# Opening loads on the sync queue in order of use, and new order lists for all engines, in an adaLN + expert + SwiGLU kernel

## What is computed

```python
def layer0(x, mu):                       # mu: cond_512, 64 numbers per sequence
    U = (mu @ W_dec + b_dec).reshape(B, 129, 30)
    param = einsum('bik,kj->bij', U, V)
    y = einsum('bsd,bde->bse', x, param[:, :-1]) + param[:, -1][:, None]
    gate = y @ Wg.T + bg                 # top 2 of 8 experts, softmax of the two
    o = gelu(y @ W1[e].T + b1[e]) @ W2[e].T + b2[e]
    return x + sum(w[e] * o[e] for e in top2)

def layer1(x):                           # norms with table rows by token, three state MLPs
    c = mlp_ln(concat(w0*h, w1*t, w2*m, w3*n, w4*r, w5*s))
    g = silu(w1(c)) * w2(c)
    return x + w3(gelu(h2(gelu(h1(g)))))
```

## Time and profile before

| | |
|---|---|
| median of 3 runs | 432.87 us (432.76 to 434.07) |
| the profiled execution | 432.91 us |
| its span | 431.1 us |
| PE busy | 413.5 us, 96% |
| DVE, ACT, POOL busy | 73%, 68%, 27% |
| moved by DMA | 45.07 MB |

### The profile page before, as it was taken

The page is one execution under the profiler, slowest core; times in us unless marked ns, Lnnn a source line. Parts: engine busy times, 40 slices in busy tenths (PEclk is TensorE's granted clock), DMA queues, the critical chain, the costliest instruction groups (busy, mean ns, idle before and its releaser), DMA issues.

```text
span 431.1 us, 5758 instructions
## 1 busy us (share of the span) xinstructions
PE 413.5 (96%) x1812; PEld 270.2 (63%) x1812; DVE 312.8 (73%) x656; ACT 292.0 (68%) x518; POOL 115.0 (27%) x122
## 2 busy tenths in 40 slices
PE   8698899999999999999999999999999999898996
PEld 5475455544656765776567665776577556677774
DVE  5489999987995587658866657678864788666653
ACT  4378967877756874677746884686668474857654
POOL 0026401443426520244153000448035031110000
PEclk9999999999999999999999999999999999999999
DMA  7976637563453342324531160325502210000000
GB/s 235 361 326 175 191 102 190 131 177 98 134 122 106 105 127 65 105 52 119 150 92 38 49 172 2 87 62 172 164 0 65 73 56 0 2 0 26 0 24 27
DMA packets 30216, 45.07 MB, mean 105 GB/s; under 512 B 3717, under 2 KB 22634, under 8 KB 29674
## 3 DMA queue, kind: packets, MB, share of 16 engines
q1 hardware_dynamic: 25504, 32.82, 26.4%
q0 software_dynamic: 3584, 10.49, 7.5%
q10 hardware_dynamic: 1098, 1.40, 1.1%
HBM read 40.68 MB, written 4.03 MB: 104 GB/s over the span
## 4 chain that ended last, share of the span: by engine, by line
PE 78%; DVE 9%; DMA 4%; issue 4%; ACT 3%; ACTq 1%; POOL 1%; SPq 1%; DVEq 0%
PE bank L750 21%; PE bank L648 20%; PE bank L786 7%; PE bank L696 7%; PE bank L640 6%; PE bank L735 5%; PE bank L664 2%; PE bank L703 2%; DMA keepP<-keepP_in 2%; DMA t_split<-tsS 2%; PE bank L775 1%; DVE mG L1190 1%; ACT mG L899 1%; PE bank L555 1%; DVE bn L1199 1%
## 5 line engine op out<-in xcount | busy, mean ns | idle before, releaser
L648 PE MATMUL bank<-mG,W 128*128 128x512 f32 x256 | 119.6, 593 | 0.0
L899 ACT ACTIVATE mG<-bank,keepP 128x512 f32<-128x512 f32 x128 | 85.3, 687 | 27.2 <-PE bank L640 17.6
L1464 POOL TENSOR_TENSOR rstd<-ve,mhalf 128x4 f32<-128x4 f32 x24 | 32.8, 1366 | 203.6 <-DVE ve L1205 203.5
L1190 DVE TENSOR_TENSOR mG<-mG,gwbs 128x1024 f32<-128x1024 f32 x64 | 77.3, 1218 | 2.1 <-DMA gwbs<-gate_w 1.3
L648 PEld LDWEIGHTS bank<-mG,W 128*128 128x128 f32 x256 | 47.5, 189 | 38.9 <-issue 35.3
L640 PE MATMUL bank<-ts,A 96*128 96x512 f32 x128 | 62.2, 526 | 1.7 <-ACT mG L899 1.6
L964 ACT ACTIVATE G<-bank,keepP 128x512 f32<-128x512 f32 x48 | 32.2, 692 | 27.9 <-PE bank L750 27.8
L1445 POOL DMA_INDIRECT gp<-pgb_in,ixall x32 | 35.8, 1119 | 26.7 <-issue 9.1
L750 PE MATMUL bank<-hB_h,h2w_h 128*128 128x512 f32 x96 | 39.7, 414 | 0.0
L750 PE MATMUL bank<-hA_h,h1w_h 128*128 128x512 f32 x96 | 38.7, 403 | 0.0
L1448 POOL DMA_INDIRECT gcm<-ctm,ixcm x32 | 35.1, 1098 | 9.8 <-issue 9.4
(11 more groups left out here) (243 smaller groups left out, 782.4 us busy)
## 6 DMA issues: line engine op xcount, KB each, us to landing
gwbs<-gate_w SPq DMA_DIRECT2D x32, 512.0 KB
keep<-xT_in SPq DMA_DIRECT2D x8, 256.0 KB, 6.0
outT<-keep SPq DMA_DIRECT2D x8, 256.0 KB, 2.1
t_split<-tsS SPq DMA_DIRECT2D x7, 192.0 KB
ts<-t_split SPq DMA_DIRECT2D x7, 192.0 KB
W1T<-W1T_in SPq DMA_DIRECT2D x1, 1024.0 KB, 8.7
W<-W2T_in SPq DMA_DIRECT2D x1, 1024.0 KB, 13.6
hs<-h1T_in SPq DMA_DIRECT2D x1, 1024.0 KB, 8.5
```

The lines of the kernel that those rows point to most:

```text
L648: mm = pe.matmul(OACC[:, :], W2[:, e * HC + c, :], mG[n % NMG][:, c, :], start=False, stop=(e == E - 1 and c == HC - 1))
L899: act.activation(mG[e % NMG][:, c % HC, :], HM[n % 2][:, :], ACT.Gelu, bias=b1c[:, c:c + 1]).then_inc(m_gelu, 1)
L1190: dve.tensor_tensor(mine, mine, gate.unsqueeze(1).broadcast_to([P, HC, TT, P]), ALU.mult).then_inc(m_q, 1)
L1464: step(pool.tensor_tensor(rstd[:, n, :], ve[:, n, :], mhalf[:, :], ALU.pow))
```

## The change

Three things, in the opening's loads and in the lists:

1. Loads that ACT issued (bdec, Vk, keepP, wd_u, earlyP, w12s) are issued by SP; ACT keeps the two factors in `gap`, muT and bdec_u, the last now ahead of its first activation. SP's loads stand in a new order, W1T in two parts (its first 512 columns with a semaphore of their own). wd_u shares `ld_v` with Vk and keepP, so those who wait for one wait for all three.
2. The lists of all five engines are new, in every block. The weights are split in another order (w12, w3, h2, h1).
3. The change is said to have "seven products without readers". `WARM` and the four `fi` are the same in both programs; the `fi` stand at other places.

```diff
             load(Wd[:, :], A["W_dec"][:, 0:KR * D].rearrange("m (h c) -> m h c", h=2), ld_wd)
+            load(bdec, A["b_dec"][:, 0:KR * D].rearrange("o (i k) -> (o i) k", k=KR), ld_bd)
             load(keep[0][:, :], A["xT"][:, 0:T], x_in[0])
-            load(W1T[:, :], A["W1T"], ld_W1T)
+            load(Vk[:, :], A["V"], ld_v)
+            load(keepP[:, :], A["keepP"], ld_v)
+            load(wd_u, A["W_dec"][:, KR * D:KR * (D + 1)].unsqueeze(1).broadcast_to([MU, 2, KR]), ld_v)
+            load(W1T[:, 0:T], A["W1T"][:, 0:T], ld_W1T)
+            load(earlyP[:, :], A["earlyP"], ld_small)
+            load(keep[1][:, :], A["xT"][:, T:2 * T], x_in[1])
+            load(states[:, :, :], A["states"], ld_state)
+            load(earlyB[:, :], A["earlyB"].partition_broadcast(P), ld_state)
             sp.wait_ge(setup0, 1)
...
+            load(keep[2][:, :], A["xT"][:, 2 * T:3 * T], x_in[2])
+            load(W1T[:, T:], A["W1T"][:, T:], ld_W1T_rest)
+            load(xTr[0][:, :], A["xT"][:, 3 * T:5 * T], ld_x[0])
+            load(xTr[1][:, :], A["xT"][:, 5 * T:8 * T], ld_x[1])
...
-            load(W2[:, :, :].rearrange("p n d -> p (n d)"), A["W2T"], ld_w2)
-            load(w3s[:, :], A["w3T"], ld_w[3])
             sp.wait_ge(u_even, 4)
             sp.wait_ge(u_odd, 4)
             load(h1s, A["h1T"], ld_w[1])
+            load(W2[:, :, :].rearrange("p n d -> p (n d)"), A["W2T"], ld_w2)
             load(h2s, A["h2T"], ld_w[2])
+            load(w12s[:, :], A["w12T"], ld_w[0])
+            load(w3s[:, :], A["w3T"], ld_w[3])
             run(steps, ORDER["SP"])
...
                 elif n == 1:
+                    pe.wait_ge(ld_W1T_rest, 16)
                     pe.wait_ge(u_odd, 1)
...
-            load(wd_u, A["W_dec"][:, KR * D:KR * (D + 1)].unsqueeze(1).broadcast_to([MU, 2, KR]), ld_wu)
-            load(bdec, A["b_dec"][:, 0:KR * D].rearrange("o (i k) -> (o i) k", k=KR), ld_bd)
-            load(Vk[:, :], A["V"], ld_v)
-            load(keepP[:, :], A["keepP"], ld_v)
-            load(earlyP[:, :], A["earlyP"], ld_small)
+            load(bdec_u, A["b_dec"][:, KR * D:KR * (D + 1)].rearrange("o k -> k o"), ld_bd)
             act.wait_ge(setup0, 1)
             act.activation(warmA[:, 0:64], onesf[:, 0:64], ACT.Copy)
-            load(bdec_u, A["b_dec"][:, KR * D:KR * (D + 1)].rearrange("o k -> k o"), ld_bd)
...
-            load(w12s[:, :], A["w12T"], ld_w[0])
...
-            dve.wait_ge(ld_wu, 16)
+            dve.wait_ge(ld_v, 48)
```

Of the lists, SP's of block 0 and PE's of block 6:

```diff
-                (0, "sgw0 sgp0 sts1 gb0 lr gb1 +lt sts2 sts3 gb2 gb3 sgw1 sgp1"),
+                (0, "sts1 sgw0 sgp0 sts2 gb0 +lt lr gb1 gb2 gb3 sgw1 sgp1"),
...
-                (6, "H0 -O5 H1 H2 ~F1 H3 =Ts H4 -O6 =Th H5 ~F2 H6 -O7 =Z B H7 ~F3 O0 H8 H9 -XT =Y ~F4 ~F5 ~F6 ~F7 H10 O1 H11 =YT O2 "
-                    "H12 ~F8 ~F9 ~F10 ~F11 H13 O3 O4 ~F12 H14 =F0 -Tt H15"),
+                (6, "H0 H1 =Ts -O5 H2 H3 =Th ~F1 H4 -O6 -O7 ~F2 =Z ~F3 -XT H5 H6 =Y B O0 H7 ~F4 ~F5 ~F6 ~F7 H8 -Tt H9 O1 =YT O2 H10 "
+                    "~F8 ~F9 H11 H12 ~F10 ~F11 H13 O3 H14 O4 ~F12 H15 =F0 -Ts"),
```

More of the change, by code:

```diff
@@ L222, in build @@
         CT = nc.dram_tensor("ctm", [A["ctg"].shape[0] * A["msg"].shape[0], 3 * P], F32, kind="Internal").ap()
-        ld_v, ld_wd, ld_wu, ld_bd, ld_small, ld_W1T, ld_const, ld_state = sems("ld_v", "ld_wd", "ld_wu", "ld_bd", "ld_small", "ld_W1T", "ld_const", "ld_state")
+        ld_v, ld_wd, ld_bd, ld_small, ld_W1T, ld_W1T_rest, ld_const, ld_state = sems(
+            "ld_v", "ld_wd", "ld_bd", "ld_small", "ld_W1T", "ld_W1T_rest", "ld_const", "ld_state")
         ld_x = sems("ld_x0", "ld_x1")
@@ L305, in weights_done @@
         def weights_done(eng, *ns):
-            eng.wait_ge(w_lo, max((4, 2, 1, 3)[n] for n in ns))
+            eng.wait_ge(w_lo, max((4, 3, 2, 1)[n] for n in ns))
         def wide(v, n):
@@ L332, in build @@
             "ACT": (
[19 rows of a table removed]
[19 rows of a table added]
             ),
             "DVE": (
[14 rows of a table removed]
[15 rows of a table added]
             ),
             "POOL": (
-                (0, "tcl0 ix tcl1 tcl2 tab0 srt tab1 tab2 tab3 rt0"),
-                (1, "tab0 -rt1 tab1 tab2 rt0 tab3 -rt2 rt1"),
-                (2, "tab0 tab1 tab2 rt0 tab3"),
-                (3, "tab0 =rt2 -rt1 tab1 tab2 tab3 rt0"),
-                (4, "tab0 =rt2 tab1 -rt1 tab2 tab3"),
-                (5, "tab0 -rt0 tab1 tab2 =rt2 -rt1 -rt2 tab3 rt0 rt1"),
-                (6, "tab0 tab1 tab2 tab3"),
-                (7, "tab0 -rt0 -rt1 =rt2 tab1 tab2 -rt2 tab3 rt0 rt1 rt2"),
[8 rows of a table added]
             ),
             "SP": (
[8 rows of a table removed]
[4 rows of a table added]
+                (4, "gb0 ^stored -lx -li gb1 gb2 +lt gb3 +lr ~stored #lt"),
[3 rows of a table added]
             ),
@@ L428, in _ @@
                 load(dst, A[src], ld_state)
-            load(states[:, :, :], A["states"], ld_state)
-            load(earlyB[:, :], A["earlyB"].partition_broadcast(P), ld_state)
+            load(keep[2][:, :], A["xT"][:, 2 * T:3 * T], x_in[2])
+            load(W1T[:, T:], A["W1T"][:, T:], ld_W1T_rest)
+            load(xTr[0][:, :], A["xT"][:, 3 * T:5 * T], ld_x[0])
+            load(xTr[1][:, :], A["xT"][:, 5 * T:8 * T], ld_x[1])
             nm, nc_ = A["msg"].shape[0], A["ctg"].shape[0]
@@ L520, in _ @@
                      "sgp": lambda i, g: store_parts(g), "vts": lambda i: store_terms(), "vtl": lambda i: load_terms()}
-            for b in (1, 2):
-                load(keep[b][:, :], A["xT"][:, b * T:(b + 1) * T], x_in[b])
-            load(xTr[0][:, :], A["xT"][:, 3 * T:5 * T], ld_x[0])
-            load(xTr[1][:, :], A["xT"][:, 5 * T:8 * T], ld_x[1])
-            load(W2[:, :, :].rearrange("p n d -> p (n d)"), A["W2T"], ld_w2)
-            load(w3s[:, :], A["w3T"], ld_w[3])
             sp.wait_ge(u_even, 4)
@@ L829, in _ @@
                 if k == 20:
-                    pe.wait_ge(ld_v, 32)
+                    pe.wait_ge(ld_v, 48)
                     pe.transpose(bank[7][:, 384:384 + KR], Vk[:, :], ident[0:KR, 0:KR]).then_inc(vt_mm, 1)
@@ L1107, in wl @@
                 src, dst = staged[n], split[n]
-                dve.wait_ge(w_hi, (3, 1, 2, 4)[n])
+                dve.wait_ge(w_hi, (1, 4, 3, 2)[n])
                 dve.tensor_tensor(flat(dst[1]), src, flat(dst[0]).bitcast(F32), ALU.subtract).then_inc(w_lo, 1)
@@ L1135, in sq_ @@
             def sq_():
-                dve.wait_ge(ld_v, 32)
+                dve.wait_ge(ld_v, 48)
                 step(dve.tensor_tensor(pair[:, :], ident[0:32, 0:BB], ident[0:32, BB:2 * BB], ALU.add))
```

## The result

The changed kernel took 440.54 us in the median of seven runs (439.08 to 447.22), the kernel before 432.87 in seven of its own (432.18 to 434.56): a ratio of 1.017, interval 1.013 to 1.022. It is slower, where I forecast 427.2.

A forecast was written before the change was run, and what follows sets the result against it. TensorE, busy 413.5 of 431.1 us, was taken as the bound, so only idle or reduced-clock time could go: 432.9 - 3.9 - 0.3 - 1.5 = 427.2 us, range 424.0 to 430.2.

The forecast's parts named there:

- Steps 1 and 2: Opening: b_dec's last part issued early, VectorE adds at 10.6, PE's 3.9 us standstill and 0.3 before L831 go.
- Step 3: Opening, 18 to 24 us: without a standstill no lower clock level, saving some 1.5 us.
- Step 4: SP's queue in the opening: seven further loads delay small constants some 4.5 us, costed at nothing.
- The sum of steps 1 to 4: Opening savings of 3.9 and 0.3 us from waits and 1.5 from the clock, taking 432.9 to 427.2 us.
- Step 5: New lists, all blocks: work after the first tm moves forward whole; reordering counted zero, up to 2.8 us either way.
- B: Block 0: gate weights land late behind other SP loads, giving back 2.6 us, 429.8 us; chance 0.18.
- D: Blocks 3 to 7: PE stops for turned norms and Z, 1.2 us in six blocks, 7.2 total, 434.4; chance 0.05.
- C: Standstill moves from L826 to block 0's first H, so nothing arrives at the end: 432 us; chance 0.04.
- E: The "seven products without readers" name something the diff doesn't alter; time stays 427.2; chance 0.53 together with the forecast.

The follow-up runs named there:

- experiment 3: The kernel before with one line moved: the load of b_dec's last 30 numbers becomes ACT's third issue; 430.06 us, ratio 0.994.
- experiment 1: The changed kernel's new opening loads with the lists and weight-split order of the kernel before; 429.48 us, ratio 0.991.
- experiment 10: The changed kernel with old lists in blocks 0 to 2 (SP's to block 3), VectorE's =flo moved before -hg in block 2; 431.30 us, ratio 0.995.
- experiment 5: The changed kernel with the load of B's gate parts (lr) moved right behind gb0 in SP's block 1 list only; 436.90 us, ratio 1.009.
- experiment 12: experiment 5 with ScalarE's low-part sums (lc) moved, two one place earlier in block 1 and two in block 2; 435.09 us.
- experiment 7: experiment 1 with two more products without a reader, behind the first two tm and ahead of the second A; 429.41 us.
- experiment 4: The changed kernel with gate-weight stores and the gate-part load (lr) ahead of split-token stores in SP's blocks 0 and 1; 443.44 us, ratio 1.025.

## Why the prediction was wrong

**Steps 1 and 2, b_dec and the standstill: right.** VectorE's adds start at 10.51 (10.6 foretold), A at 15.45 (15.5), tm0 at 16.53 (16.5). b_dec's last part landed at 6.9 (issued at 2.07, 4.8 us to landing), earlier than the 10.3 I took; nothing hung on the difference. The DMA issues of the change:

```profile
gap<-b_dec_in SPq DMA_DIRECT2D x1, 15.0 KB, 5.0
...
gap<-b_dec_in ACTq DMA_DIRECT2D x1, 0.1 KB, 4.8
```

**Step 3, the clock: right with the old lists, wrong with the new.** I expected no lower level once the standstill was gone. With the old lists that is what happened in most runs (mean clock 0.999 in experiment 3, 0.996 to 1.000 in three of four of experiment 1, against 0.993 of before). With the new ones it came at 19.66, with a stop of only 1.05 us beside it, and lasted 6.8 us instead of 3.4. In two profiles with the old lists in block 0 it fell there too (6.8 us from 20.8 in experiment 1's slowest run, 3.4 from 21.8 in experiment 10), so the new lists aren't needed for it. The rule of the Trainium skill that I cited (TensorE: Matmul & The Clock Gate, HAM oscillation) prices the time at the lower level by one half; the trace agrees (17.1 us more of it, 8.5 lost, 8.8 measured as busy time). What I didn't ask is what else would pull the clock down.

**Step 4, later loads on SP: right.** Neither PE nor VectorE waited for W1T, W2 or the constants in the opening. The rule on turns between queues (the Trainium skill, DMA: Bandwidth & Descriptors, Queues, rings and completion order) spoke against moving small loads onto SP. That loss didn't show: b_dec's main part landed 5.0 us after its issue on SP, where on ACT's queue it had taken 8.4. It is no test of the rule itself, since the time of issue and the loads ahead on the same queue changed too.

**The sum of steps 1 to 4** was -5.7; experiment 1 measured -3.6 in the median and -4.9 in its one run at a mean clock of 1.000 (428.24). So some 0.8 is a shift that doesn't reach the dense part whole (experiment 3's profile shows 0.4 of it: the first tm starts 4.4 us earlier and the execution ends 4.0 earlier), and the rest goes with smaller falls of the clock that most runs still have somewhere.

**How much of the lists' 11.0 is clock.** (1 - mean clock) times the span, in the median of each kernel's runs, is 1.1 us in experiment 1 and 5.5 in the change: an estimate of 4.4 us for the clock, if all slow work lies on the path, and of 6.6 for the stops themselves. It fits the change's own runs: 439.08 at 0.989 to 447.22 at 0.971, all between 434.3 and 435.0 once that part is taken off. It doesn't fit everywhere: the nine runs of experiment 5 come to 430.8 to 434.3 by the same sum, so there the clock is only a part of the spread.

**Step 5, "I take zero, as the dense part can't gain": this is the step that failed.** I costed new lists on all five engines at nothing, with a range of 2.8 us to both sides, out of the largest waits of the old trace. They cost 11.0. The first half of the step failed as well, that the work behind the first tm "moves forward as a whole": from the first tm to the gates' first store it took 10.4 us before, 14.0 in the change (5.0 us won shrank to 1.4). The argument looked only at what a list can gain. What it can lose isn't bounded by the waits of before, since every position that hides something today may be given up. The loss lies in the blocks up to 110 us, 9.2 of 11.0 us. There VectorE had been 81 to 98% busy and ScalarE 57 to 97% in windows of 10 us from 20 to 100; that a list has little to spare where its engines are nearly full is my reading, and no run shows it. What the runs assign:

- 3.6 us: the load of the gate parts behind stores in SP's block 1 (experiment 5), with the low clock beside its stop.
- 5.6 us: the rest in blocks 0 to 2 (436.9 against 431.3). ScalarE's low-part sums, crowded into block 2, may be up to 1.8 of it (experiment 12), but this isn't shown. The profile of experiment 12 has single waits of 0.3 to 1.2 us for gelus, for YN (1.05) and tT (1.1), and one of 0.9 for OG; no run took one of these away alone, so this stays open, as does VectorE's wait of 1.71 for gwbs in the change.
- 1.8 us: blocks 3 to 7 (experiment 10 against 1); which step in them isn't settled either.

**The rivals.** *B* named the right mechanism, a transfer for the gates behind other work on SP, for the weights gwbs in block 0 and at 2.6 us. Its sign came: gwbs was awaited in block 0, 1.71 us, though its store wasn't held by the loads, which SP had all issued by 18.7, but came late with the gate steps; what this wait costs no run tells. What is shown to cost is the parts, OG, in block 1, at 3.6. I had in hand the list with `lr` behind `sts3 vts sts4 gb1 +lt`, and didn't follow the queue beyond block 0. *D* was the slower case, with stops of PE in blocks 3 to 7 from turned norms and Z; its place was wrong. In those blocks the change runs nearly parallel to before (11.4 us late at block 3, some 12 at block 7), and the stops came in the first three, with SP's and ScalarE's work. Its chance of 0.05 was too small for any loss from five new lists. *C* has a grain of truth, the shift that arrives short. *E* is so: nothing in the time points to products without readers.

## What to carry over

New order lists are a change of their own: cost them from both sides, and walk each queue past the first block, asking for every load that PE needs what now stands before it. A reordering can lose far more than the waits shown can give back: here 11.0 us against 2.8. Where a change bundles loads and order, exchange the two halves first; here two runs split -3.6 from +11.0, and one moved line held most of the gain, so the version to keep is the new loads (or b_dec's line alone) with the old lists.

## What wasn't expected of the hardware

- **A load of 120 bytes held VectorE for 5.9 us and PE for 3.9**: 11.0 us from issue to landing as ACT's eighth load, and 6.2 (experiment 3) and 4.8 (the change) as its third.
- **Short stops can be followed by a low clock, and its length varies.** Rows of this case: 3.4 us after waits of 0.86 and 0.87 (experiment 7, from 47.3), 10.2 from within one of 3.12 (the change, from 70.9), 13.65 after 2.84 (experiment 4), and none after 0.98 in experiment 3. The same stop in front of the first gate product (L583, 1.05 or 1.06 us) has 6.8 us beside it in the change, 3.4 in experiment 5 and none in experiment 12. PE's timelines of experiments 5 and 12, where the four passes of A behind it take 3.43 and 1.96:

```profile
19.86 1.22 PE L583 MATMUL bank<-G,tT 32*128 32x8 f32 x8 [1.06 <-DVE tT L1152]
21.01 3.43 PE L823 MATMUL bank<-W1T,gap 128*96 128x512 f32 x4
```

```profile
19.87 1.05 PE L583 MATMUL bank<-G,tT 32*128 32x8 f32 x8 [1.06 <-DVE tT L1152]
20.85 1.96 PE L823 MATMUL bank<-W1T,gap 128*96 128x512 f32 x4
```

  The same program differs from run to run: experiment 5 ran from 434.4 us at a mean clock of 0.993 to 441.4 at 0.981, while before, with its one long stop, stayed within 2.4 us. In these runs the lists with many small stops of PE were not only longer but less steady.
- **Beside PE's stop and the lower clock the other engines idle too.** In the change from 70 to 80 us (window above) ScalarE was busy 2.35 of 10 us and VectorE 5.01; in experiment 5, where the stop at 71 us and the slow clock are gone, 8.19 and 8.73. The two windows hold the stop and the clock together and not quite the same work, so their shares aren't told apart:

```profile
70.00:80.00 10.00, 8.89 (x30) 4.65 (x28) 8.73 (x19) 8.19 (x17) 4.77 (x5) 1.00 0.72 168
```
